# Sowing four routed tiles instead of eight, and fetching the last chunk by itself, in an attention and expert layer on one core

## The reference, cut to what matters

```python
x = x + attn(_layernorm(x))                       # causal, head dimension 1024
h = _layernorm(x)
scores = softmax(h @ gate_w.T)
top_scores, sel = top_k(scores, 2)                # 4096 tokens, 8192 rows
order = argsort(sel.T.reshape(-1), stable=True)   # rows sorted by expert
y = (silu(x_sorted @ w1[e]) * (x_sorted @ w3[e])) @ w2[e]
out = zeros.at[tok_sorted].add(y * scores_sorted) # two rows for each token
x = x + out
```

## Time and profile before

| | |
|---|---|
| median of 3 runs | 242.02 us (241.62 to 243.9) |
| profiled execution, span from first to last instruction | 240.8 us |
| median less span (start and end of the launch) | 1.2 us |
| TensorE, VectorE, POOL busy | 230.1, 186.3, 164.7 us |
| POOL's indirect DMAs | 64 scatters, 64 stores |
| start of the last store, its landing | 226.10 us, 228.45 us |
| last VectorE instruction ends | 238.51 us |

### The profile page before, as it was taken

How to read it: one execution, slowest core, us unless ns; L and a number is a source line. 1 busy time by engine, 2 the same in 40 slices (tenths; PEclk the granted TensorE clock), 3 DMA queues, 4 the chain that set the end, 5 groups by cost and what they waited for, 6 DMA issues and landing times.

```text
span 240.8 us, 6517 instructions
## 1 busy us (share of the span) xinstructions
PE 230.1 (96%) x1822; PEld 209.0 (87%) x1823; DVE 186.3 (77%) x848; ACT 145.7 (61%) x391; POOL 164.7 (68%) x204
## 2 busy tenths in 40 slices
PE   7989999999999999999999999899999999999945
PEld 6967878788789867776999999889999999999934
DVE  2489898879897889977898799667766666699835
ACT  2267777777877766854799666555566565656100
POOL 6523337788888888868587787777777777788500
PEclk9999999999999999999999999999999999999997
DMA  6999701101111111133034336433333333796374
GB/s 230 313 323 328 207 4 35 46 26 45 34 49 35 48 45 46 37 72 107 27 93 103 97 97 146 127 96 109 106 102 102 97 99 99 231 356 184 107 259 133
DMA packets 31947, 28.89 MB, mean 120 GB/s; under 512 B 4137, under 2 KB 26545, under 8 KB 31921
## 3 DMA queue, kind: packets, MB, share of 16 engines
q1 hardware_dynamic: 26448, 19.39, 29.1%
q0 software_dynamic: 4096, 8.53, 10.5%
q10 hardware_dynamic: 1376, 0.66, 0.9%
HBM read 16.34 MB, written 12.22 MB: 119 GB/s over the span
## 4 chain that ended last, share of the span: by engine, by line
PE 79%; DMA 6%; POOL 4%; DVE 3%; issue 3%; ACT 2%; ACTq 1%; POOLq 1%; SPq 0%; DVEq 0%
PE weighed L649 12%; PE scores L594 12%; PE turned L722 11%; PE scores L722 11%; PE turned L619 6%; PE scores L743 5%; PE mixed L607 3%; PE mixed L608 3%; PE mixed L743 3%; PE weighed L743 3%; DMA choice_rows<-ysb,ycol 2%; POOL expert_rows L503 2%; DMA XX<-choice_rows 2%; DMA TL<-L_attn_w_o 1%; PE scores L583 1%
## 5 line engine op out<-in xcount | busy, mean ns | idle before, releaser
L514 POOL DMA_INDIRECT choice_rows<-ysb,ycol x64 | 66.1, 1033 | 19.5 <-issue 12.8
L503 POOL DMA_INDIRECT expert_rows<-rows,slots x64 | 64.5, 1008 | 18.2 <-issue 12.7
L860 ACT ACTIVATE Wt<-W 128x512 f32 x71 | 44.0, 624 | 15.8 <-issue 15.8
L722 PE MATMUL scores<-xT,Wt 128*128 128x128 f32 x288 | 38.1, 275 | 0.6 <-issue 0.6
L649 PE MATMUL weighed<-TL,PT 128*128 128x136 f32 x272 | 37.0, 281 | 0.4 <-DVE X L984 0.3
L594 PE MATMUL scores<-XX,TL 128*128 128x512 f32 (+3 forms) x96 | 36.7, 491 | 0.7 <-ACT XX L822 0.5
L722 PE MATMUL turned<-xT,Wt 128*128 128x128 f32 x280 | 37.1, 275 | 0.0
L722 PEld LDWEIGHTS scores<-xT,Wt 128*128 128x128 f32 x288 | 35.0, 192 | 0.8 <-issue 0.8
L649 PEld LDWEIGHTS weighed<-TL,PT 128*128 128x128 f32 x272 | 33.7, 190 | 1.1 <-issue 0.8
L722 PEld LDWEIGHTS turned<-xT,Wt 128*128 128x128 f32 x280 | 34.1, 192 | 0.0
L972 DVE TENSOR_REDUCE negmax<-scores 128x1 f32<-128x128 f32 (+7 forms) x32 | 23.5, 735 | 5.4 <-PE scores L595 5.4
(11 more groups left out here) (184 smaller groups left out, 464.8 us busy)
## 6 DMA issues: line engine op xcount, KB each, us to landing
xt<-expert_rows SPq DMA_DIRECT2D x71, 66.0 KB, 2.0
XX<-choice_rows SPq DMA_DIRECT2D x16, 256.0 KB, 4.5
W<-L_ffn_w SPq DMA_DIRECT2D x2, 1024.0 KB, 9.7
out<-X SPq DMA_DIRECT2D x9, 128.0 KB
X<-L_attn_in_features SPq DMA_DIRECT2D x2, 512.0 KB, 8.0
expert_rows<-rows,slots POOLq DMA_INDIRECT x64, 2.5
choice_rows<-ysb,ycol POOLq DMA_INDIRECT x64, 2.3
out<-X ACTq DMA_DIRECT2D x5, 128.0 KB
```

Source lines behind the costliest of these rows:

```text
L503: nc.gpsimd.indirect_dma_start(xs, bass.IndirectOffsetOnAxis(ap=slots[:, u, k:k + 1], axis=0), rows[:, u % ROWS_RING, k, :], None).then_in ...
L514: nc.gpsimd.indirect_dma_start(yb, bass.IndirectOffsetOnAxis(ap=ycol[:, q, 0:1].bitcast(u32), axis=0), ysb[:, q, :], None).then_inc(y_out[ ...
L722: mm(bank[2 + j % RING][:, c * P:(c + 1) * P], Wt[:, j % RING, c * P:(c + 1) * P], xT[:, j % RING, :], start=True, stop=True)
L860: copy(Wt[:, j % RING, :], W[:, ds(w * (SET // WIDE), SET)], ACT.Copy).then_inc(Wt_rdy, 1)
```

## The change

The second list gets a fourth level: after the tiles that are full after group 6 come those full after 30 of the 32 token tiles, then the rest. For that, `ranks` counts the last group also without its last two token tiles (three more small matmuls), VectorE copies one more count, and the vectors of `list_rest` have 32 segments instead of 24, so 40 x 32 = 1280 numbers. By this order the routed tiles 67 to 70 can hold only rows of the last two token tiles. So 67 routed tiles are stored (three more, behind POOL's loop) and four are sown, each with two matmuls into one bank and a 0/1 matrix of 128x256; `clear` is gone. SP's fetches of chunks 5 and 6 now wait for the routed tiles 0 to 62 instead of 0 to 63. Chunk 7 is fetched after that, when all 67 are stored: choice 0 by SP, choice 1 by ACT. It is added by halves of two token tiles (four operations of 128x256), each half written out when it is done; the sown sums go into the second half before. `add_choice(5, 1)` moves behind the result of routed tile 69.

Left out here are the tiles' and semaphores' declarations, an assertion, and POOL's constants with the sizes that follow.

```diff
--- before.py
+++ after.py
@@ -59,12 +59,14 @@
 NEAR = 16
-FAR, LATER = 6, 64
-LEVELS = (HALF, FAR, len(GROUPS) - 1)
+FAR, LATER = 6, 63
+SOWN = 2
+LEVELS = (HALF, FAR, len(GROUPS) - 1, len(GROUPS) - 1)
 SEG = len(LEVELS) * E
...
 assert (K * P * sum(n for _, n in GROUPS[:FAR + 1]) + E * (P - 1)) // P <= LATER
+assert GROUPS[-1][1] > SOWN
 N_PARTS = 5
...
@@ -79,14 +81,15 @@
 SOW_LAG = 5
-BY_PE = 7
-STORED = NT - BY_PE
+STORED = (K * P * (N_TILES - SOWN) + E * (P - 1)) // P
+BY_PE = NT - STORED
 NF = N_TILES // FIN
...
 ADD_AT = [59, 61, 62, 64, 65]
+REST_OF = (STORED // OUT_LANES, STORED % OUT_LANES)
...
@@ -314,6 +317,10 @@
+        def sown_at(i):
+            return (ACC[0], 0) if i < SOWN - 2 else (ACC[1], (i - SOWN + 2) * D)
         def pair_bank(t):
...
@@ -324,8 +331,25 @@
-        assert pair_bank(LAST_TURN - 1) == 6 and pair_bank(LAST_TURN - 2) == 7 and LAST_TURN + 2 == STORED + SOW_LAG
+        assert pair_bank(LAST_TURN - 1) == 6 and pair_bank(LAST_TURN - 2) == 7 and STORED >= LAST_TURN - LAG
         assert all(pair_before(t) == t - RING for t in range(LANES, LAST_TURN + 1))
+        def stores_in(eng, t0, t1):
+            for q in range(OUT_LANES):
+                if len(range(q, t1, OUT_LANES)) > len(range(q, t0, OUT_LANES)):
+                    eng.wait_ge(y_out[q], 16 * len(range(q, t1, OUT_LANES)))
+        def fetch_last(eng, k):
+            eng.wait_ge(sum1, LAST - ZF + 1)
+            eng.dma_start(yf[:, LAST % ZF, k, :, :], yv[:, k, LAST, :, :]).then_inc(yf_in[LAST % ZF], 16)
+        def write_last(eng, h):
+            n, z = pieces(LAST)[h]
+            eng.wait_ge(last1, h + 1)
+            eng.dma_start(ov[:, n:n + z, :], X[:, n:n + z, 0:D]).then_inc(out_done, 16)
...
@@ -419,14 +443,12 @@
                 write(c)
-            for q in range(OUT_LANES):
-                sp.wait_ge(y_out[q], 16 * len(range(q, LATER, OUT_LANES)))
-            for c in range(N_EARLY, NF):
+            stores_in(sp, 0, LATER)
+            for c in range(N_EARLY, LAST):
                 fetch(c)
-
-            sp.wait_ge(sum2, 1)
-            n, z = pieces(LAST)[0]
-            sp.dma_start(ov[:, n:n + z, :], X[:, n:n + z, 0:D]).then_inc(out_done, 16)
+            stores_in(sp, LATER, STORED)
+            fetch_last(sp, 0)
+            write_last(sp, 0)
             sp.wait_ge(out_done, 16 * sum(len(pieces(c)) for c in range(NF)))
...
@@ -569,6 +591,8 @@
                     store(r, q)
+            for q in range(REST_OF[1]):
+                store(REST_OF[0], q)
...
@@ -633,6 +657,11 @@
                     mm(RANKS[:, n * E:(n + 1) * E], onesb[:, :], counted[:, gr + 1, 0, :], start=True, stop=True)
+                if gr == NG - 1:
+                    for b in range(n - SOWN + 1):
+                        mm(RANKS[:, (n + 1) * E:(n + 2) * E], onesb[:, :], counted[:, gr, b, :], start=b == 0,
+                           stop=b == n - SOWN)
                 mm(R_, onesb[0:1, :], stretchb[:, 0:1, :].to_broadcast([1, n, E]), start=True, stop=False)
...
@@ -650,23 +679,17 @@
-            def clear():
-
-                pe.wait_ge(y_rdy, LAST_TURN - LAG)
-                for a in ACC:
-                    mm(a[:, 0:2 * D], onesb[:, :], counted[:, 0, 0:1, :].to_broadcast([P, 2 * D // E, E]),
-                       start=True, stop=False)
-
             def sow(t):
...
                 pe.wait_ge(pick_rdy, n + 1)
-                for i in range(FIN):
-                    o = mm(ACC[i // 2][:, i % 2 * D:(i % 2 + 1) * D], pick[n][:, i * P:(i + 1) * P], ysb[:, t % OUT_LANES, :],
-                           start=False, stop=n == BY_PE - 1 and i % 2 == 1)
-                    if n == BY_PE - 1 and i % 2 == 1:
-                        o.then_inc(sown_mm, 1)
+                for i in range(SOWN):
+                    a, at = sown_at(i)
+                    o = mm(a[:, at:at + D], pick[n][:, i * P:(i + 1) * P], ysb[:, t % OUT_LANES, :],
+                           start=n == 0 and at == 0, stop=n == BY_PE - 1, skip_group_check=True)
+                if n == BY_PE - 1:
+                    o.then_inc(sown_mm, 1)
...
@@ -759,8 +782,6 @@
                 pair(m, j, w[LIST0 + j - LAG])
-                if static and t == STORED + SOW_LAG:
-                    clear()
                 if static and t >= STORED + SOW_LAG:
...
@@ -807,8 +828,9 @@
             for t in range(NT - LAG, NT):
-                sow(t - 2)
                 pair(*divmod(t + LAG, LANES), w[LIST0 + t % LANES])
+                if t - 2 >= STORED:
+                    sow(t - 2)
             sow(NT - 2)
...
@@ -925,13 +947,13 @@
+            stores_in(act, 0, STORED)
+            fetch_last(act, 1)
             for c in range(N_EARLY, N_LATER):
...
                     act.dma_start(ov[:, n:n + z, :], X[:, n:n + z, 0:D]).then_inc(out_done, 16)
-            act.wait_ge(sum2, 2)
-            n, z = pieces(LAST)[1]
-            act.dma_start(ov[:, n:n + z, :], X[:, n:n + z, 0:D]).then_inc(out_done, 16)
+            write_last(act, 1)
...
@@ -1046,7 +1068,10 @@
                 if gr in LEVELS:
-                    link(v.tensor_copy(cnt[:, LEVELS.index(gr), :], RANKS[0:1, n * E:(n + 1) * E]))
+                    link(v.tensor_copy(cnt[:, NL - 1 if gr == NG - 1 else LEVELS.index(gr), :],
+                                       RANKS[0:1, n * E:(n + 1) * E]))
+                if gr == NG - 1:
+                    link(v.tensor_copy(cnt[:, NL - 2, :], RANKS[0:1, (n + 1) * E:(n + 2) * E]))
                 v.tensor_tensor(picked[:, gr % 2, 0:n, :, :], hot[:, a:a + n, :, :],
...
@@ -1380,20 +1405,32 @@
                         picks(STORED + 2 * (t - NT + LEAD) + n)
-            for t in range(NT - LAG, NT):
-                out_pair(*divmod(t + LAG, OUT_LANES))
-                if t == NT - LAG:
-                    for k in range(K):
-                        add_choice(N_EARLY, k)
-            for c in range(N_EARLY + 1, NF):
-                for k in range(K):
-                    add_choice(c, k)
+            out_pair(*divmod(NT, OUT_LANES))
+            add_choice(N_EARLY, 0)
+            out_pair(*divmod(NT + 1, OUT_LANES))
+            add_choice(N_EARLY, 1)
+            out_pair(*divmod(NT + 2, OUT_LANES))
+            for k in range(K):
+                add_choice(N_EARLY + 1, k)
+            n1 = N_TILES - SOWN
+            dve.wait_ge(sown_mm, 1)
+            for i in range(SOWN - 2):
+                v.tensor_tensor(X[:, n1 + i, 0:D], X[:, n1 + i, 0:D], ACC[0][:, i * D:(i + 1) * D],
+                                ALU.add).then_inc(sum2, 1)
+            v.tensor_tensor(X[:, N_TILES - 2:, 0:D], X[:, N_TILES - 2:, 0:D],
+                            ACC[1][:, 0:2 * D].rearrange("p (n d) -> p n d", d=D), ALU.add).then_inc(sum2, 1)
+            dve.wait_ge(yf_in[LAST % ZF], 16 * K * (LAST // ZF + 1))
             for h, (n, z) in enumerate(pieces(LAST)):
-                dve.wait_ge(sum1, NF)
-                dve.wait_ge(sown_mm, h + 1)
-                v.tensor_tensor(X[:, n:n + z, 0:D], X[:, n:n + z, 0:D],
-                                ACC[h][:, 0:z * D].rearrange("p (n d) -> p n d", d=D),
-                                ALU.add).then_inc(sum2, 1)
+                at = n - CHUNKS[LAST][0]
+                if h == 1:
+                    dve.wait_ge(sum2, 1)
+                v.tensor_tensor(X[:, n:n + z, 0:D], X[:, n:n + z, 0:D], yf[:, LAST % ZF, 0, at:at + z, :],
+                                ALU.add).then_inc(last0, 1)
+                dve.wait_ge(last0, h + 1)
+                v.tensor_tensor(X[:, n:n + z, 0:D], X[:, n:n + z, 0:D], yf[:, LAST % ZF, 1, at:at + z, :],
+                                ALU.add).then_inc(last1, 1)
```

More of the change, by code:

```diff
@@ L192, in build @@
         ysb, ycol = sb("ysb", [P, OUT_LANES, D]), sb("ycol", [P, OUT_LANES, COL_W + 1 - COL_DEST])
-        place_of_tok = sb("place_of_tok", [P, FIN, P])
+        place_of_tok = sb("place_of_tok", [P, SOWN, P])
         lowi, lowf = sb("lowi", [P, BY_PE], u32), sb("lowf", [P, BY_PE])
-        pick = [B_[:, h, n * FIN * P:(n + 1) * FIN * P] for B_ in (Pr, PT) for h in range(2) for n in range(2)]
+        pick = [B_[:, h, n * SOWN * P:(n + 1) * SOWN * P] for B_ in (Pr, PT) for h in range(2) for n in range(2)]
         yf = XX[:, 0:ZF * K * FIN, :].rearrange("p (z k i) d -> p z k i d", z=ZF, k=K)
@@ L236, in build @@
             sem("y_zero"), sem("low_rdy"), sem("lowf_rdy"), sem("pick_rdy"), sem("sown_mm"))
-        sum2 = sem("sum2")
+        sum2, last0, last1 = sem("sum2"), sem("last0"), sem("last1")
         assert NF - N_EARLY == LAG
@@ L292, in build @@
         assert not any(wide(u) and u % 2 for u in range(N_TILES - XT_LEAD))
-        RANKS = pM[:, 0:(MOST + 1) * E]
+        RANKS = pM[:, 0:(MOST + 2) * E]
         LAST_SLOT = N_TILES - 1 + LANES
@@ L299, in build @@
         assert RANK_LAG <= LANES
-        assert LATER == STORED and BY_PE <= len(pick) and FIN * P == 512
+        assert BY_PE <= len(pick) and STORED // OUT_LANES == (NT - 1) // OUT_LANES
         LAST = NF - 1
```

(2 more changed lines are left out.)

## The result

The changed kernel takes 243.61 us (median of 20 runs, one of which took 348.59). The kernel before, timed beside it on the same chip, takes 241.67 (20 runs). The ratio is 1.0074 with a 95% interval of 1.0054 to 1.0094, so the change costs 1.8 us (1.3 to 2.3). Ratios here leave out executions more than 1.5% above the fastest one of their kernel, so a ratio can differ by some tenths of a per cent from that of the two medians beside it. The change lies inside 1%, as forecast, and inside the range; but the forecast moved to the wrong side of no change, and the interval excludes it.

What follows compares the result with a forecast made beforehand. The prediction took POOL's delayed stores to set the end: last store at 230.37, landed 233.17, chunk 7 at 236.61, additions to 238.37, write to 240.66. Carrying over 1.22 from span to median gave 241.9 us, range 240.2 to 244.2.

Steps and rivals of the forecast that it cites:

- What bounds the kernel: POOL's delayed stores reach the end through last landing, fetch and additions; TensorE's last sowings are a second path.
- Steps 1 to 3: Start of POOL's last store: longer list +0.57, fewer 0/1 matrices -0.1, three more stores +3.80, from 226.10 to 230.37.
- step 1: Longer list: two VectorE operations with two SBUF inputs each hold a POOL store 0.29 longer, +0.57; bounds 0 and 1.4.
- 2-port rule: By the skill, picks beside POOL's last three stores would hold them 1.5; the forecast took 0.1 from the profile row.
- Step 4: Landing of POOL's last store beside the fetches of chunks 5 and 6: 2.8 us, bounds 2.35 and 5.1.
- late landing: POOL's last store waits behind the fetches of chunks 5 and 6, landing up to 5.1: 244.2 us; chance 0.1.
- Step 5: Fetch of chunk 7 in two halves, 512 KB side by side: 3.3 us, bounds 2.0 and 4.5.
- no quicker than the others: Rival: chunk 7's fetch takes 4.5 instead of 3.3, since ACT's writes cross it: 243.1 us; chance 0.1.
- "slower" rival: Stores 64 to 66 run into the fetches of chunks 5 and 6; last landing 2.3 longer: 244.2 us; chance 0.1.
- the case of both together: Last store lands late and chunk 7's fetch is slow: 245.4 us, within the 0.09 given to times above 244.4.
- The rival with a stall of TensorE: VectorE's longer list stalls TensorE instead of falling into its wait, up to 1.6 on all: 243.5 us; chance 0.05.
- Steps 6 and 7: After chunk 7's fetch: four additions of 128x256, 1.76 us, then the last write, 2.29 us, to 240.66.

Runs made afterwards that it cites:

- thin additions: Kernel before, with the additions of chunks 0 to 4 cut to one column of 128; 239.82 us, ratio 0.9922.
- end-alone kernel: Changed kernel with the old list of three levels and without the extra count; 243.17 us, ratio 1.0065 to the kernel before.
- results-first kernel: Kernel before, tiles 69 and 70 ahead of chunk 5's additions, sown sums before chunk 7, chunks 5 and 6 fetched after tile 62; 241.62 us, ratio 1.0015.
- ACT's writes late: Changed kernel, but ACT writes chunks 5 and 6 only after chunk 7 has landed; 244.54 us, ratio 1.0105 to the kernel before.
- one queue: Changed kernel with SP issuing both halves of chunk 7, ACT writing chunks 5 and 6 once summed; 244.37 us, ratio 1.0095 to the kernel before.
- the list alone: Kernel before with only the list's fourth level, its 1280 numbers and the extra count; 242.47 us, ratio 1.0011.

## Why the prediction was wrong, point by point

**What bounds the kernel: right.** POOL's last store, its landing and the last fetch set the end; taking holds away from POOL moved the end (thin additions), and TensorE's sowing, halved by the change, gave nothing back. Its last eight matmul records took 2.08 us and not 0.8, since the granted clock stood at 0.50 (1.2 GHz) after 4.79 idle, and ended at 236.10, not before 236; the wait for chunk 7 covered that.

**Steps 1 to 3, start of the last store: the prices were right, but one term was missing.** The two stores beside the long list took 2.07 and 1.97; the forecast had 2.0 and 1.9. The three more stores cost 3.80, as forecast. But beside the additions of chunks 0 to 4 the stores were held by 2.3 in all instead of 3.2 before, which nothing in the forecast says. That comes from the phase: three additions in a row began only after their stores had started (from 211.20 on) and held nothing. It is chance from one execution to the next, since in the end-alone kernel, with the same additions, the holds sum to 1.25, and in the results-first kernel to 3.25. So the store started 0.74 ahead of the forecast, from the first scatter on, and the sum carried over from its rows one draw of a term that varies by 2 us. That its start in the trace came within 0.43 of the forecast is in part luck: the trace itself starts 0.31 late. The rate of step 1, 0.86 us for each us of overlap, is not how the hold works: it is what the operation still has to run when the store starts, less 0.13. For an operation that grows by 0.33 the two give nearly the same.

The picks cost POOL little, as forecast: with the additions thinned, the last two stores, beside picks, took 1.19 and 1.08, so the 2-port rule of the Trainium skill ("GPSIMD Engine Reference", Key points) shows no large hold here either. Its rule on two SBUF inputs holds, for operations that are running when the store starts.

**Step 4, the landing: the term that failed.** The forecast took 2.8 from a store with writes beside it, between bounds of 2.35 and 5.1. It was 4.83. The other kernels sort by the fetches issued ahead of the last store: 4.83, 4.54, 4.27 and 4.36 with 1 MB, 2.59 with 512 KB, and 2.35, 2.64 and 2.54 with none. The last group is not as tight as these three: the last store of the kernel with thinned additions took 3.30, and in the trace before, the store at 223.47, one ahead of the one that the forecast took its 2.8 from, landed after 3.9 with writes only. The argument against the late landing was that the 1 MB is "gone by about 232.3". Most of it was, and it did not help. DMA share and GB/s (the last two columns) of the changed kernel:

```profile
231.00:232.00 1.00, 1.00 1.07 402
232.00:233.00 1.00, 0.60 0.31 119
233.00:234.00 1.00, 0.50 0.06 25
234.00:235.00 1.00, 0.50 0.02 8
```

From 233 some 25 GB/s move at a share of 0.06, which is one of 16 engines, until 234.2; the store counts as landed at 234.77. In the kernel with ACT's writes late, the fetches were issued only from 228.83, the traffic went on into the microsecond from 233 and stopped, and the store landed at 234.21:

```profile
232.00:233.00 1.00, 1.00 1.02 393
233.00:234.00 1.00, 0.99 0.45 172
234.00:235.00 1.00, 0.50 0.00 0
```

In both, the landing comes within a microsecond of the end of all traffic; a store alone lands after some 2.5 us. What the store waits for can be read from the packets of POOL's queue, 32 for each store, in the traces:

| kernel | last store starts | packets of POOL's queue, beside those of the fetches | lands |
|---|---|---|---|
| before | 226.10 | 32 in 227.5 to 228.5, with no fetch | 228.45 |
| ACT's writes late | 229.67 | 1 in 231.6 to 232.5, beside 192; 32 from 232.5 on | 234.21 |
| one queue | 230.18 | none in 232.0 to 233.1, beside 208; 32 from 233.1 on | 234.54 |
| changed | 229.94 | none in 231.0 to 231.8, beside 163; 58 of the last two stores' in 231.8 to 232.6, the last few until after 234 | 234.77 |

A store alone moves its data from 1.4 us after its start. With 1 MB of fetches ahead they move only 2.8 and 2.9 after it, when the fetches' are nearly through. The Trainium skill, "DMA: Bandwidth & Descriptors", Queues, rings and completion order, says two things on that. A DMA engine takes turns between its queues, by which a store would lose little; the stretches without a packet of POOL's do not look like that. And the write that raises a semaphore lands only after every earlier write of that DMA engine, across its queues. That may add to the wait, but can't be all of it here, since the store's own data come late already. Why POOL's queue stands still beside the fetches, and why in the changed kernel one engine goes on for some 1.6 us after the others, no run here shows.

**Step 5, the last fetch: also too low**, 4.08 against 3.3. The rival "no quicker than the others" had named the cause, ACT's writes that cross it: 3.92, 3.98, 4.08 and 4.22 with the four writes, 3.49 without. Its 4.5 was too high, for the crossed fetches too. The fetch took more than 4, which the prediction had named as a sign of being wrong. The estimate of 3.2 by "DMA: Bandwidth & Descriptors" of the Trainium skill (a fit for DMAs that GpSimd issues, while these go out on SP and ACT) is near the fetch with nothing across it, 3.49, and far from the others.

**The rivals.** The "slower" rival was the right mechanism. Its price, the landing less 2.8, is 2.03 here, and it decides past 2.9, as written. I gave it 0.1, and the slow fetch 0.1. They have different causes, the fetches ahead of the store and ACT's writes across the last fetch: without the fetches of chunks 5 and 6 the landing was short and the fetch slow (2.54, 4.22), with ACT's writes late it was the other way round (4.54, 3.49). The change brings both causes, so both came, and the case of both together stood only in the 0.09 above 244.4. Both forecast and rival bounds held the truth; the fault is the middle value, which I took from a store beside lighter traffic, though the change itself puts four stores behind the one that releases the fetches. The rival with a stall of TensorE did not come: the list alone is within 0.9 us of nothing.

**Steps 6 and 7: right**, 1.70 and 2.31. The 1.22 carried from span to median was 0.6 too small (244.81 less 243.0 is 1.8), which bears on both kernels alike.

**Why removing the fetches gained 1.2 by the runs.** From the first scatter on, its profile gains 2.0: the landing 2.29, less a fetch that is 0.14 slower and a last store that starts 0.12 later, where the moved additions hold the store ahead of it by 0.34. The 2.0 lies at the upper end of the runs' interval (0.4 to 2.0), so whether anything is left to explain stays open.

## What to carry to other kernels

When a change puts stores behind the start of large fetches, take the landing of the last store from a row with that traffic beside it, not from a quieter one: 1 MB ahead made 2.5 into 4.3 to 4.8 us. Where the change brings the causes of two rivals at once, the two together are a case of their own, with their prices added. Before two traces are compared, count from a common event; 36.28 to 38.59 for the first scatter is more than the whole effect here. Against a store engine without gaps, results first, two-input additions moved away from the stores, and the fetch issues split over two queues together gained 0.6%, where shortening TensorE's tail gained nothing.

## What the runs showed of the hardware

- A DMA's making on POOL that starts while VectorE runs an operation with two SBUF inputs takes longer by what that operation still has to run, less 0.13 us (118 of 120 cases in the fourteen traces). One that had 0.33 to run held a store by 0.20, one with 0.92 by 0.79, one with 1.23 by 1.11.
- The same operation held nothing when it began after the DMA's making had (22 cases, 0.95 to 0.97 us each). So the same pair of long operations (1x1280) held POOL's DMAs by 1.11 and 1.01 in one kernel and by 0.13 and 1.02 in another, and the holds of a run of additions summed to 1.25 in one execution and 3.25 in another.
- With the additions cut to one column of 128, nothing was held (0.95 to 0.96 for the nine stores from 209.55 to 219.65), with the same transfers in flight.
- With 1 MB of fetches issued ahead, POOL's queue moved 0 and 1 packets in 1.1 and 0.9 us, while the fetches moved 208 and 192; the store's data came 1.5 us later than alone.
- A fetch of 512 KB on two queues took 3.49 alone and 3.92 to 4.22 when four writes of 128 KB crossed it.
